# A one-layer decoder: batch 0's residual, norm and queries moved up; the experts' down projections in three passes; rows of the experts' blocks loaded by two engines

## The chip, the cores and the metric

The kernel runs on one core of one Trainium2 chip. The metric is the device time of one execution in microseconds; lower is better. The time before is the median of three runs.

## The reference

The layer has a width D of 256, 16 heads of 16, 32 sequences of 112 tokens, and a context of 375 positions for each sequence. All is float32:

```python
x = x + self_attention(layernorm(x))        # causal, window of 64
x = x + cross_attention(layernorm(x), ctx)  # bias by relative position, 375 keys
x = x + experts(layernorm(x))

# experts: 8 of them, each token goes to its best two
probs = softmax(xf @ router_w.T); keep the top 2, normalise them
g = xf @ gate_w[e] + gate_b[e]; u = xf @ up_w[e] + up_b[e]
h = silu(g) * u                              # 512 wide
y = sum over the two experts of prob * (h @ down_w[e] + down_b[e])
```

## The kernel before

Each engine runs its own instruction stream, and all streams are made from one list of steps. A step is a name and a batch number (`("x1", 0)`), and it stands for one piece of work on one engine; semaphores tie the streams together. `order(B)` builds the list: a periodic order for the 32 batches (`PERIOD`), then an order written out by hand for the end of the attention part and the first part of the experts (`TAIL_ORDER`).

**Attention, about the first 865 us.** Per batch: norm, queries and keys, masked scores in four groups (`sm0` to `sm3` on VectorE, 16 small reductions with the mask, and `su` on GpSimd behind them), values, output projection (`wo`), residual (`x1`), norm (`ln2`, `rs2` on GpSimd, `xn2` on ScalarE), its transpose (`x2T`, copied by `x2Tc`) and the cross queries (`q2`, split into a rounded high part by `q2m` on ScalarE and a low part by `q2l` on VectorE). The two halves of the queries are then paired by a DMA (`qx`), without which the first cross scores (`S0`) can't start. The cross keys (`k0`, `k1`) are split in the same way by `k0c` and `k1c` (ScalarE) and `k0l` and `k1l` (VectorE). The steps of these small products take the two PSUM banks A and B in turn, in the order of the list; a step waits until the one that had the bank before it is drained. For `k0` and `k1` that is when `k0l` and `k1l` are done. `split_weights` splits the context's weights, once, at step `cl` of batch 0.

**Experts.** Token rows are scattered to DRAM by expert (`sc`), and read back in blocks of 128 rows that all belong to one expert. The first 42 blocks (`NFULL`) are worked on in 21 pairs (`NP`), the last 21 one by one. `blocks:n` are small VectorE steps that compute the table of blocks. `get` and `add_and_load` on GpSimd load the rows of a block into one of `XB` = 12 buffers; `add` adds a block's result to the output in DRAM by an indirect DMA, which waits until the results before it have landed. Per pair k, TensorE transposes the rows of pair k+1, does the gate product (step `bg`), the up product (`bu`) and then the down product of pair k-1 (`down_pair`, L916). Gate and up products of a pair run in the format fp32r: weights and rows are each split into a high part (ScalarE copies it) and a low part (VectorE subtracts), and three products (`PASSES`: high x high, low x high, high x low) make up one float32 product (L901). The down product is a plain float32 product, which the trace shows as two instructions each. In the last 21 blocks all three products are plain float32 (L866, L876). VectorE weighs the result (`weigh_rows`, L1420) into one of two buffers `y2`. TensorE's down product waits in the next round until VectorE has read the last one (`s_yw`).

The order of VectorE in a pair is: `weigh_pair`, the up weights' low part, the low part of the next rows, and in step `bu` the next gate weights' low part and four multiplications into `hidden_rows`. ScalarE: the up weights' high part, the copy of the next rows, the activation of the gate, the next gate weights' high part, the weighted bias.

## Time and profile before

| what | us |
|---|---|
| median of 3 runs | 1214.28 (1214.12 to 1214.49) |
| the profiled execution, its own time | 1211.85 |
| its span | 1210.2 |
| TensorE busy (matmul) in the span | 1168.2 (97%) |
| VectorE, ScalarE, GpSimd busy | 868.3, 753.8, 821.0 |

The profile is of one execution. Its table in 40 slices has TensorE at nine tenths or more from the third slice on but for one; the stages before and after differ in what the other engines do beside it.

### The profile page before, as it was taken

The page shows a single profiled execution, that of the slowest core. Times are in us where ns is not written, and L with a number is a line of the kernel's source. Part 1 is how long each engine was busy: PE and PEld are TensorE (multiplying, and loading weights), DVE is VectorE, ACT ScalarE, POOL GpSimd, SP SyncE. Part 2 cuts the span into 40 slices and gives each one's busy share as a digit, 9 for nine tenths or more (in the row PEclk, how much of TensorE's full clock was granted, in tenths as well). Part 3 has the DMA queues.
Part 4 walks back from the last instruction along what each step waited for, and adds up shares of the span by engine and source line. Part 5 has one row for each costly group of instructions (what it writes and reads, how often), then busy time and mean ns, then how long its engine had stood idle before and what let it go on. Part 6 is the DMA issues. An engine that isn't in the chain of part 4 may idle for free.

```text
span 1210.2 us, 36900 instructions
## 1 busy us (share of the span) xinstructions
PE 1168.2 (97%) x12874; PEld 1023.7 (85%) x12874; DVE 868.3 (72%) x3851; ACT 753.8 (62%) x1845; POOL 821.0 (68%) x1593
## 2 busy tenths in 40 slices
PE   6899999999999999999999999999899999999996
PEld 4688888888888888888888888887689999998995
DVE  3567888888888888888888888888777655544442
ACT  2567766767766767766766766766564555555552
POOL 4677788778788778788778788876636644444432
PEclk8999999999999999999999999999899999999998
DMA  8411122121122121112112112122765433333221
GB/s 191 93 43 47 50 59 75 50 58 58 51 58 75 50 58 58 51 59 75 52 58 59 51 58 71 48 65 87 230 212 140 76 57 54 53 58 56 46 32 23
DMA packets 70936, 86.11 MB, mean 71 GB/s; under 512 B 25600, under 2 KB 57728, under 8 KB 70752
## 3 DMA queue, kind: packets, MB, share of 16 engines
q1 hardware_dynamic: 54768, 58.60, 16.7%
q0 software_dynamic: 15552, 25.05, 10.7%
q8 instruction: 105, 1.72, 0.6%
q14 instruction: 79, 0.65, 0.2%
q10 hardware_dynamic: 432, 0.10, 0.0%
HBM read 43.10 MB, written 20.95 MB: 53 GB/s over the span
## 4 chain that ended last, share of the span: by engine, by line
PE 90%; DVE 4%; issue 2%; POOL 2%; DMA 1%; ACT 0%; POOLq 0%; DVEq 0%
PE bank_S L901 10%; PE bank_Q L824 7%; PE bank_P L824 6%; PE bank_Q L916 5%; PE bank_S L815 5%; PE bank_S L866 5%; PE bank_B L737 4%; PE bank_A L737 4%; PE bank_B L837 4%; PE bank_A L837 3%; PE bank_A L804 3%; PE bank_P L763 3%; PE bank_B L804 3%; PE bank_Q L876 3%; PE bank_B L796 3%; PE bank_S L754 3%
## 5 line engine op out<-in xcount | busy, mean ns | idle before, releaser
L628 POOL TENSOR_SCALAR arena<-arena,mC 112x375 f32<-112x375 f32 x512 | 297.6, 594 | 26.4 <-DVE mC L1282 24.3
L1282 DVE CUSTOM_DVE_ANT_0 arena<-bank_S,arena 112x375 f32<-112x375 f32 x512 | 260.4, 543 | 56.9 <-PE bank_P L824 30.4
L634 POOL TENSOR_SCALAR arena<-arena 112x112 f32<-112x112 f32 x512 | 175.0, 356 | 85.3 <-DVE arena L1270 85.3
L654 POOL DMA_INDIRECT out<-y,xb x63 | 106.6, 1692 | 83.8 <-DVE y L1420 48.6
L824 PE MATMUL bank_Q<-ident,arena 112*126 112x112 f32 x858 | 131.9, 262 | 2.1 <-POOL arena L628 1.5
L1071 ACT ACTIVATE pTC<-bank_P 126x336 f32<-126x336 f32 x226 | 102.6, 454 | 40.6 <-PE bank_P L824 16.9
L1270 DVE CUSTOM_DVE_ANT_0 arena<-bank_S,arena 112x112 f32<-112x112 f32 x512 | 102.1, 270 | 14.6 <-PE bank_S L754 14.6
L1071 ACT ACTIVATE pTC<-bank_Q 126x336 f32<-126x336 f32 x222 | 101.3, 456 | 18.1 <-PE bank_Q L824 14.6
L824 PEld LDWEIGHTS bank_Q<-ident,arena 112*126 112x126 f32 x858 | 96.2, 141 | 15.4 <-issue 9.7
L824 PE MATMUL bank_P<-ident,arena 112*126 112x112 f32 x678 | 107.9, 268 | 1.3 <-ACT pTC L1071 0.8
L647 POOL DMA_DIRECT2D xb<-xs x63 | 44.1, 700 | 80.1 <-issue 76.6
L824 PEld LDWEIGHTS bank_P<-ident,arena 112*126 112x126 f32 x678 | 74.7, 140 | 26.1 <-issue 16.1
L641 POOL DMA_INDIRECT xs<-x,pos x64 | 65.6, 1025 | 26.1 <-issue 22.3
L815 PE MATMUL bank_S<-k,q 32*112 32x376 f32 x1024 | 77.1, 374 | 3.7 <-issue 2.7
L916 PE MATMUL bank_Q<-arena,hidden_rows 128*128 x336 | 76.0, 379 | 0.0
L916 PEld LDWEIGHTS bank_Q<-arena,hidden_rows 128*128 128x128 f32 x336 | 62.4, 190 | 7.6
L1431 DVE TENSOR_TENSOR gwR_low<-arena,gwR_high 128x1024 fp32r<-128x1024 f32 x21 | 26.1, 1243 | 48.4 <-ACT gwR_high L1120 45.0
L614 POOL TENSOR_TENSOR rstd<-rstd,power 112x1 f32<-112x1 f32 x96 | 54.6, 568 | 8.0
L613 POOL TENSOR_SCALAR rstd<-mv 112x1 f32<-112x1 f32 x96 | 22.3, 233 | 55.5 <-DVE mv L1250 50.4
L1410 DVE SCALAR_TENSOR_TENSOR hidden_rows<-bank_S,gub,gates 128x128 f32<-128x128 f32 x84 | 23.7, 345 | 48.7 <-PE bank_S L866 42.4
L815 PEld LDWEIGHTS bank_S<-k,q 32*112 32x112 f32 x1024 | 35.4, 170 | 27.2 <-issue 21.0
L1035 ACT ACTIVATE arena<-bank_A 128x224 f32<-128x224 f32 (+2 forms) x102 | 43.6, 428 | 19.8 <-PE bank_A L745 7.7
(263 smaller groups left out, 3566.9 us busy)
## 6 DMA issues: line engine op xcount, KB each, us to landing
arena<-in_l_ctxT SPq DMA_DIRECT2D x32, 378.0 KB, 3.5
k<-k_low SPq DMA_DIRECT2D x64, 188.0 KB, 2.3
xb<-xs POOLq DMA_DIRECT2D x63, 129.0 KB
q<-q SPq DMA_DIRECT2D x64, 112.0 KB
arena<-in_L_ffn_gate_w SPq DMA_DIRECT2D x8, 512.0 KB
arena<-in_L_ffn_up_w SPq DMA_DIRECT2D x8, 512.0 KB
arena<-in_L_ffn_down_w SPq DMA_DIRECT2D x8, 512.0 KB
arena<-in_x SPq DMA_DIRECT2D x32, 112.0 KB, 2.0
```

Of the source, the lines that this page charges most:

```text
L628: pool.tensor_scalar(z[n % NZ][:, 0:T], z[n % NZ][:, 0:T], -1.0, mC[:, n:n + 1], ALU.mult, ALU.add).then_inc(s_u, 1)
L634: m = pool.tensor_scalar(sF[r][:, j, :], sF[r][:, j, :], -1.0, mF[:, r, j:j + 1], ALU.mult, ALU.add)
L654: pool.indirect_dma_start(out=out[:, :], out_offset=bass.IndirectOffsetOnAxis(ap=xb[x][:, D + 1:D + 2].bitcast(I32), axis=0), in_=y2[x % 2 ...
L737: m = pe.matmul(dst, xt[:, c, :], w[:, c, 0:n], start=(c == 0), stop=(c == DC - 1))
L815: m = pe.matmul(bank[f"S{r}"][0:S, 0:T + 1], q2[b % 2][32 * r:32 * r + 32, u, c, p, :], k2[b % 2][32 * r:32 * r + 32, c, p, :], start=u == ...
L824: m = pe.transpose(B_[0:TP, t * S:(t + 1) * S], z[n % NZ][:, t * TP:(t + 1) * TP], ident[0:S, 0:S])
L837: m = pe.matmul(B_[32 * r:32 * r + HP, 0:S], v2[b % 2][:, t, n, :], pTC[n % NZ][:, t, :], start=(t == 0), stop=(t == TC - 1))
L901: m = pe.matmul(bk[f // 2][:, f % 2 * 2 * P:(f % 2 + 1) * 2 * P], wR[part][w][:, c, f * P:(f + 1) * P], xbR[k % 2][u][:, c, :], start=(c = ...
L916: m = pe.matmul(bankY[:, h * D:(h + 1) * D], hidden_rows[k % 2][:, c, h * P:(h + 1) * P], w[:, c, :], start=(c == 0), stop=(c == FC - 1))
L1071: act.activation(pTC[n % NZ][:, :, :], v3(B_, TC, S, TP), ACT.Exp).then_inc(drain_sem(f"p{n}", b), 1)
L1270: m = dve.tensor_tensor_reduce(out=sF[r][:, j, :], in0=t[:, j, :], in1=window[:, :], scale=1.0, scalar=3.0e38, op0=ALU.add, op1=ALU.min, a ...
L1282: dve.tensor_tensor_reduce(out=z[n % NZ][:, 0:T], in0=bank[f"S{r}"][0:S, 0:T], in1=nbias[:, n, :], scale=1.0, scalar=3.0e38, op0=ALU.add, ...
```

## The change

1. **Beginning.** A table `BEGINNING` moves nine steps of batch 0 in the list: `rs2`, `x1`, `ln2`, `xn2`, `x2Tc`, `q2m`, `q2l`, `q2` and `x2T`. `split_weights` moves from `cl` to `nrm` of batch 0, and the copy of a constant from batch 0's `x1` to batch 1's.
2. **Down products in three passes.** The down weights and the hidden values are split into high and low parts as the others are. One buffer of each (`wR["dw"]`, `hR`), and one `hidden_rows` where there were two. Blocks 42 and 62 keep the plain product.
3. **Loads.** 10 row buffers where there were 12. GpSimd loads the rows for the first four pairs' adds (`SEAM` = 8), then SyncE does it. Odd pairs up to 17 write their results to `xbT`, so that there are four result buffers.
4. **Order of the end.** `warm` (the first gate weights' split) and the transpose `x3T` of batch 30 go behind the last softmax steps and `pv3`; the block table's parts are spread over more pairs, one in each.

Cut to its core:

```diff
-XB = 12
+XB = 10
+SEAM = 8
+BEGINNING = (("rs2", 0, ("su3", 1)), ("x1", 0, ("sm3", 1)), ("ln2", 0, ("sm3", 1)), ("xn2", 0, ("k1c", 0)),
+             ("x2Tc", 0, ("k1c", 0)), ("q2m", 1, ("k1c", 0)), ("q2l", 1, ("k1l", 0)), ("q2", 1, ("k1", 0)), ("x2T", 1, ("k1", 0)))
 def order(B):
+    for word, behind, anchor in BEGINNING:
+        steps.remove((word, 0))
+        steps.insert(steps.index(anchor) + behind, (word, 0))
...
-p15 e14 warm pv2 oc1 e15 p13 oc2 p12 e13 pf:-2 e12 pkg:10 ... pfD:-2 rcB:-2
-x3T:-1 x3Tc:-1 pv3 oc3 bt otc ...
+p15 e14 pv2 oc1 e15 p13 oc2 p12 e13 pf:-2 e12 warm pkg:10 ... pfD:-2 rcB:-2 pv3 oc3 x3T:-1
+x3Tc:-1 bt otc ...
...
+            hR = [sb(f"hR_{part}", [P, FC, 2 * P], F32R, st) for part in ("high", "low")]
+            rows_out = [[y2[h] if k % 2 == 0 or k > NP - 4 else xbT[h] for h in range(2)] for k in range(NP)]
@@ SyncE
+                    def load_behind(j):
+                        sp.wait_ge(s_add, 16 * (j - (j > NFULL)))
+                        for n in (j + XB - 2, j + XB - 1) if j < NFULL else (j + XB - 2,):
...
+                                load_rows(n)
...
@@ TensorE
                     def down_pair(k):
-                        pe.wait_ge(s_hh, 2 * k + 2)
+                        pe.wait_ge(s_dw, k + 1)
+                        pe.wait_ge(s_hl, k + 1)
...
-                                m = pe.matmul(bankY[:, h * D:(h + 1) * D], hidden_rows[k % 2][:, c, h * P:(h + 1) * P], w[:, c, :],
+                                for u, w in PASSES:
+                                    m = pe.matmul(bankY[:, h * D:(h + 1) * D], hR[u][:, c, h * P:(h + 1) * P],
...
@@ ScalarE, step bg
+                    def hidden_high(k):
+                        act.wait_ge(s_hh, 2 * k + 2)
+                        if k:
+                            act.wait_ge(s_y, 2 * k)
+                        act.activation(hR[0][:, :, :], hidden_rows[:, :, :], ACT.Copy).then_inc(s_hi, 1)
...
+                            if b:
+                                hidden_high(b - 1)
+                                weights_high(b - 1, "dw", s_y)
                             for half in range(2):
                                 silu_pair(b, half)
@@ VectorE, step bg
                                 copy_low(b + 1)
+                            if b:
+                                hidden_low(b - 1)
+                                weights_low(b - 1, "dw", s_dw, 1)
...
@@ VectorE, single blocks
                     for j in range(NFULL, NBLK):
                         if j == NFULL:
                             weigh_pair(NP - 2)
+                            hidden_low(NP - 1)
+                            weights_low(NP - 1, "dw", s_dw, 1)
+                        elif j > NFULL + 1:
+                            down_low(j - 1)
                         if j + 1 < NBLK:
                             weights(j + 1)
                         hidden(j)
...
@@ VectorE, weigh_rows
-                        if j >= 2:
-                            dve.wait_ge(s_add, 16 * (j - j % 2 if j < NFULL else max(j - 1, NFULL)))
+                        if j >= NFULL:
+                            dve.wait_ge(s_add, 16 * max(j - 1, NFULL))
+                        elif j // 2 > NP - 3:
+                            dve.wait_ge(s_add, 16 * (j - j % 2))
+                        elif j >= 4:
+                            dve.wait_ge(s_add, 16 * (j - j % 2 - 2))
```

## Rows read from the trace of the kernel before

**Rows 1.** The page's first part: busy us, share of the span, instructions.
```profile
PE 1168.2 (97%) x12874; PEld 1023.7 (85%) x12874; DVE 868.3 (72%) x3851; ACT 753.8 (62%) x1845; POOL 821.0 (68%) x1593
```
**Rows 2.** Windows: length, busy PE, PEld, DVE, ACT, POOL, PEclk, DMA share, GB/s.
```profile
929.31:1064.37 135.06, 135.06 (x954) 128.56 (x953) 80.04 (x147) 73.04 (x127) 72.54 (x63) 1.00 0.37 63
```
**Rows 3.** The chain that ended last, one pair: start us, us, what.
```profile
987.19 3.46 PE bank_Q L916 x16
991.09 5.75 PE bank_S L901 x48
996.84 3.46 PE bank_Q L916 x16
```
**Rows 4.** The same chain, one single block.
```profile
1103.31 3.57 PE bank_S L866 x32
1106.88 1.73 PE bank_Q L876 x8
```
**Rows 5.** Timeline of DVE over one pair; in brackets the idle time before.
```profile
986.62 1.23 DVE L1431 TENSOR_TENSOR gwR_low<-arena,gwR_high 128x1024 fp32r<-128x1024 f32 x1 [2.97 <-ACT gwR_high L1120]
987.76 1.65 DVE L1442 SCALAR_TENSOR_TENSOR hidden_rows<-bank_S,gub,gates 128x256 f32<-128x256 f32 x4
990.69 0.88 DVE L1420 SCALAR_TENSOR_TENSOR y<-bank_Q,xb,dbw 128x256 f32<-128x256 f32 x2 [1.27 <-PE bank_Q L916]
991.48 1.22 DVE L1431 TENSOR_TENSOR uwR_low<-arena,uwR_high 128x1024 fp32r<-128x1024 f32 x1
992.61 0.68 DVE L1425 TENSOR_TENSOR xbR_low<-bank_P,xbR_high 128x512 fp32r<-128x512 f32 x1
```
**Rows 6.** Timeline of ACT in the same stage.
```profile
994.99 1.06 ACT L1120 ACTIVATE gwR_high<-arena 128x1024 fp32r x1
...
1000.77 0.60 ACT L1114 ACTIVATE xbR_high<-bank_P 128x512 fp32r<-128x512 f32 x1 [2.74 <-PE bank_P L888]
```
**Rows 7.** Timeline of DVE: first and last of five steps of one table part.
```profile
935.39 0.20 DVE L1370 TENSOR_TENSOR ge<-lower,nf 1x64 f32<-1x64 f32 x1
...
936.26 0.23 DVE L1375 TENSOR_TENSOR diff<-offs 1x8 f32<-1x8 f32 x1
```
**Rows 8.** Timeline of DVE in the first pairs.
```profile
923.93 0.88 DVE L1420 SCALAR_TENSOR_TENSOR y<-bank_Q,xb,dbw 128x256 f32<-128x256 f32 x2 [2.13 <-DMA out<-y,xb]
```
**Rows 9.** Timeline of POOL: adds (L654) and a load (L647).
```profile
1001.70 2.17 POOL L654 DMA_INDIRECT out<-y,xb  x1 [0.42 <-DVE y L1420]
...
1060.51 1.66 POOL L654 DMA_INDIRECT out<-y,xb  x1 [0.30 <-issue]
...
1067.55 0.60 POOL L647 DMA_DIRECT2D xb<-xs  x1 [3.49 <-issue]
```
**Rows 10.** Timeline of PE: the down product of block 43.
```profile
1095.58 1.99 PE L876 MATMUL bank_Q<-arena,hidden_rows 128*128 x8 [1.77 <-DVE y L1420]
```
**Rows 11.** Timeline of DVE at the beginning.
```profile
30.35 0.27 DVE L1270 CUSTOM_DVE_ANT_0 arena<-bank_S,arena 112x112 f32<-112x112 f32 x1
...
33.47 0.33 DVE L1470 CAST before<-x 112x112 fp32r<-112x112 f32 x1
33.83 0.42 DVE L1471 TENSOR_TENSOR x<-bank_A,arena 112x256 f32<-112x256 f32 x1
...
41.10 0.69 DVE L1487 SCALAR_TENSOR_TENSOR q<-bank_A,q 128x224 fp32r<-128x224 f32 x2 [3.39 <-ACT q L1053]
```
**Rows 12.** Timeline of PE at the beginning.
```profile
31.39 1.09 PE L737 MATMUL bank_A<-arena 128*112 128x256 f32 x4 [0.30 <-ACT arena L1035]
...
34.40 0.41 PE L796 MATMUL bank_A<-cT_high,wkv_high 128*128 128x376 f32 x1 [0.89 <-DVE x L1471]
...
45.85 0.61 PE L815 MATMUL bank_S<-k,q 32*112 32x376 f32 x8 [2.71 <-issue]
```
**Rows 13.** Windows of 1 us, PE alone: length, busy us, PEclk, DMA share, GB/s.
```profile
23.00:24.00 1.00, 0.40 (x16) 1.00 0.97 126
24.00:25.00 1.00, 0.99 (x24) 0.50 1.01 146
```

More of the change, by code:

```diff
@@ L397, in decoder_layer @@
             s_xb = [sem(f"block_loaded{i}") for i in range(XB)]
+            s_xs = [sem(f"block_loaded_by_sp{i}") for i in range(XB)]
             s_bX = sem("block_transposed")
@@ L407, in decoder_layer @@
             s_xh = sem("block_high_ready")
-            s_wh = {w: sem(f"{w}_high_ready") for w in ("gw", "uw")}
+            s_wh = {w: sem(f"{w}_high_ready") for w in ("gw", "uw", "dw")}
+            s_dw = sem("down_weights_split")
+            s_hi = sem("hidden_high_ready")
+            s_hl = sem("hidden_low_ready")
             s_db = sem("down_bias_weighted")
@@ L469, in decoder_layer, with rows_loaded @@
             filled_last = {n: max(k for m, k in place.values() if m == n) + 1 for n in "ABPQS"}
+            def rows_loaded(j):
+                first = SEAM + XB - 2
+                return (s_xb[j % XB], 16 * (j // XB + 1)) if j < first else (s_xs[j % XB], 16 * ((j - first) // XB + 1))
             held = {}
@@ L583, in _ @@
                             load_package(sp, e, half)
+                        elif step == "add" and b >= SEAM and b % 2 == 0:
+                            load_behind(b)
+                    for j in range(1 + max(b for step, b in steps if step == "add"), NBLK):
+                        if j >= NFULL or j % 2 == 0:
+                            load_behind(j)
                     sp.wait_ge(s_add, 16 * NBLK)
@@ L1119, in weights_high @@
                             act.wait_ge(used, 2 * k)
-                        act.activation(wR[part][0][:, :, :], package(e, part).rearrange("p (c f) -> p c f", c=DC), ACT.Copy).then_inc(s_wh[part], 1)
+                        act.activation(wR[part][0][:, :, :], package(e, part).rearrange("p (c f) -> p c f", f=parts[part][1] // (
+                            FC if part == "dw" else DC)), ACT.Copy).then_inc(s_wh[part], 1)
                     def silu_pair(k, half):
@@ L1232, in _ @@
                     for j in range(NFULL, NBLK):
+                        if j == NFULL:
+                            hidden_high(NP - 1)
+                            weights_high(NP - 1, "dw", s_y)
                         if j == NFULL:
@@ L1430, in weights_low @@
                         dve.wait_ge(s_wh[part], k + 1)
-                        dve.tensor_tensor(wR[part][1][:, :, :], package(e, part).rearrange("p (c f) -> p c f", c=DC), wR[part][0][:, :, :].bitcast(F32), ALU.subtract).then_inc(then, n)
+                        dve.tensor_tensor(wR[part][1][:, :, :], package(e, part).rearrange("p (c f) -> p c f", f=parts[part][1] // (
+                            FC if part == "dw" else DC)), wR[part][0][:, :, :].bitcast(F32), ALU.subtract).then_inc(then, n)
                     def hidden_pair(k, half):
@@ L1462, in _ @@
                         elif step == "nrm":
+                            if b == 0:
+                                split_weights()
                             if b:
@@ L1478, in _ @@
                         elif step == "cl":
-                            if b == 0:
-                                split_weights()
                             need(dve, s_ch, b + 1)
```

128 lines of the change are left out of this document (81 added, 47 removed).

## The prediction

> **What bounds the kernel now.** I read the page first: TensorE is busy for 97% of the span [rows 1], so the time is TensorE's work plus a few holes. Then the windows by stage. In the pair stage TensorE is busy all of 135.06 us, VectorE 80.04 of them (59%), ScalarE 73.04 [rows 2]. Then the chain of waits, which in that stage is TensorE alone: per pair 3.46 us of down product in 16 instructions, 5.75 us of gate and up products in 48, and 9.65 us from one down product to the next [rows 3]. A single block has 3.57 us of gate and up and 1.73 us of down [rows 4]. The two rows of a pair are a price list: the float32 down product has 8 products of 256 columns in 3.46 us, 0.43 us each; an fp32r product of the same 256 columns takes 5.75 / 48 = 0.12 us. Last I read VectorE's, ScalarE's and GpSimd's timelines over a pair for what stands in between [rows 5, 6, 9], and all engines' at the holes: 2.71 us before the first cross scores of batch 0 [rows 12], 1.77 us at block 43 [rows 10].
>
> **Down products in three passes.** A pair's down product becomes 24 fp32r products, 24 x 0.12 = 2.88 us for 3.46: 0.58 us less. The stationary side changes with each one, as in the rows the price is from. A single block's becomes 12 x 0.12 = 1.44 for 1.73: 0.29 us less, in 19 blocks (43 to 61), 5.5 us. The new period of a pair is 9.65 - 0.58 = 9.07 us, if TensorE stays the bound.
>
> Does it? VectorE's starts in a pair are 1.14 us apart for a low part of 128x1024, 1.57 for the four multiplications, 0.79 for weighing, 0.60 for the next rows [rows 5]; with two low parts more it has 4 x 1.14 + 1.57 + 0.79 + 0.60 = 7.5 us of 9.07. A table part adds up to 1.1 us [rows 7], in pairs 3 to 12, one each: 8.6 us. ScalarE's two more copies at 1.06 [rows 6] bring it from 5.2 (73.04 x 9.65 / 135.06) to 7.3 us. So neither is the bound by load, but the order must hold too. I set time 0 at the end of `bu`. The down product of pair k-1 ends at 2.9. VectorE weighs at 3.1 to 3.9, up weights to 5.0, rows to 5.7, and then comes `hidden_low(k)`, which needs `hidden_high(k)`: that waits for the down product (one buffer), sits behind the copy of the next rows (transposes at 3.3, copy to 4.1) and ends at 5.1; the weights' high part ends at 6.1. The low parts end at 6.9 and 8.0. TensorE comes to the down product at 9.07. The slack is 1.0 us. Behind it ScalarE has the activations and the gate weights' high part, which it ends at 8.8, so VectorE's gate weights go from 8.9 to 10.0, the multiplications to 11.6, and it can weigh at 12.2 (9.07 + 3.1): 0.5 us of slack. The 2.97 us in which VectorE waits for ScalarE now [rows 5] are the cover that the new work uses up. With a table part it is 0.5 us late, which the slack of 1.0 holds. Where that cover is gone each pair costs what it lacks. From the down product of pair 4 to that of pair 19 are 15 periods: 15 x 0.58 = 8.7 us less, and 0.6 for pair 20.
>
> **The first pairs.** There VectorE also has batch 31's routing. Beside its own order the new 2.3 us (two low parts) stand ahead of work that TensorE waits for: the up weights of pair 3 come about 1.3 us later, of pair 4 about 1.8. Against it go five cheaper down products (2.9 us), and waits of VectorE for a landed add, of which 2.13 us is the longest [rows 8]: with four result buffers they go. The swap of `x3T` and `pv3` lets `pv3` go ahead of the wait for the routing's bank, but `x3T` and behind it the first transposes of rows now wait for VectorE's first gate weights and the slot counts: the first gate product about 1 to 2 us later, half of it absorbed by VectorE's later waits. I follow the streams step by step with the durations above and get the down product of pair 4 ending 0.5 us later than before. Bounds: 3 us earlier (all down savings kept) and 4 us later (all of 2.3 us in two pairs lost).
>
> **Loads and adds.** GpSimd's cycle in a pair was two loads and two adds: from the first add to the first load behind it, which waits for both to land, 1067.55 - 1060.51 = 7.04 us [rows 9]; with the two loads behind it (0.60 each and their gaps) that is near 9, and would have been the next bound at 9.07. Without the loads it is 7.0 and 0.9 for weighing. SyncE has nothing else to do there and loads four pairs ahead, after the adds that free the buffers: nothing on the path. 10 buffers for 12 cost nothing while a load has two periods of lead.
>
> At the seam to the single blocks the result buffers are two again. From the end of pair 19's down product TensorE gets to that of block 43 in 3 x (3.57 + 0.2) + 2.88 + 1.73 = 15.9 us. The adds' chain needs 0.2 + 0.9 + 7.04 (pair 19), 0.1 + 0.9 + 7.04 (pair 20), 0.1 + 0.5 for weighing block 42, which is 16.8; and `down_low(43)` is queued on VectorE behind that weighing, 0.6 + 1.14 us more. So block 43 stalls some 2.7 us where it stalled 1.77 [rows 10]: 0.9 us lost. Bounds: 0 and 2.5.
>
> The Trainium skill ("SBUF — State Buffer", section "SBUF: two separate sides") has VectorE with two SBUF inputs and GpSimd share one port, which one of them holds for a whole instruction. The trace has a sign of it: an add issued while the up weights' low part ran took 2.17 us, others 1.66 [rows 9]. By that rule both adds of a pair can be 0.5 us longer, since VectorE now has four such instructions; 8.9 of 9.07 us, still hidden, and 1 us more at the seam, which is within its bounds.
>
> **The beginning.** The residual needs `wo`, which ends at 31.39 + 1.09 = 32.5 [rows 12]; now it starts at 33.83, after 16 masked reductions from 30.35 to 33.47 [rows 11]. Moved ahead of them it starts at 32.5: 1.3 us earlier, and VectorE stands idle before it. The norm ends at 33.6. The reductions (3.1 us) then end at 36.7, and `k0l` is queued behind them: 37.2, for about 35.4 now. But `x2T` takes bank B, which `k0` holds until `k0l`; so it runs at 37.2, its copy ends at 38.1. `k1c` is queued on ScalarE behind that copy (39.0), `k1l` follows (39.5), and `q2` takes bank A, which waits for `k1l`. `q2` and its high part take 1.8 us: `q2l` at 41.3, against 41.10 now [rows 11]. The queries come no sooner. TensorE meanwhile is idle from 34.5 to 37.2 and from 37.6 to 39.5, 4.6 us, with `qk` of batch 2 and the rest queued behind; it loses the holes of 0.89 (before `k1`) and 2.71 us [rows 12]. Net 1.0 us later at the first scores: 46.9 for 45.85. `split_weights` runs in VectorE's idle time before `nrm` and moves nothing, since `k0` comes at 32.1 for other reasons.
>
> Then the clock. After some us in which it was busy half of the time (0.40 us of the last one) the granted clock went from 1.00 to 0.50, 2.4 to 1.2 GHz [rows 13]. The new hole is emptier than that: 0.4 us of work in 5. If it falls, the 5 us of work behind it run at half speed and 2.4 us more are lost. I take 2.5 us for the whole of the beginning, bounds -1.5 (the queries 1.3 us earlier and no new hole) and 3.5.
>
> The Trainium skill ("TensorE: Matmul & The Clock Gate", section "HAM oscillation — how this bites in real kernels") says that a wait that is long enough makes the next stretch start at the low clock. By that rule the beginning costs the 3.5 us and not 1.0, and the sum would be 1204.4; it speaks against this part of the change, and the row of the fall agrees.
>
> **The sum.** First pairs 0.5, pairs -8.7 - 0.6, seam 0.9, single blocks -5.5, beginning 2.5: -10.9 us. The end is unchanged (two adds in a row behind block 62). From the profiled execution's 1211.85 that is 1201.0; the median of the runs is 2.4 above it, so 1203.4. I say 1203.
>
> **Rivals.**
> - *The beginning does what it is arranged for.* For it: VectorE reaches the residual 1.3 us earlier. Against: the banks of `k0` and `k1`. It gives 1203.4 - 4.0 = 1199.
> - *VectorE bounds the pairs.* For: 8.6 of 9.07 us in ten pairs, and waits for ScalarE between. Against: 1.0 us of slack. If each of the 15 periods is 0.3 us short: 1208.
> - *The single buffers of the split down operands, slower than before.* `hidden_high` can't start until the down product before has been read, and the low parts must end before the next: 5.1 us of chain in a window of 6.2. The price is whatever the chain has beyond 6.2, in 20 pairs. It decides against the kernel when the chain is over 6.2 + 10.9 / 20 = 6.7 us. If VectorE's wait of 2.97 us for ScalarE comes to lie ahead of the low parts and half of it is not hidden, the chain is 7.2 and the time 1203.4 + 20 x 1.0 = 1223. Against: those parts are queued ahead of that wait.
> - *The passes do not issue at 0.12 us.* If the down product saves nothing (passes at 0.144), 1203.4 + 14.8 = 1218. Against: the 48 products of a pair in the same form at 0.12 [rows 3].
>
> **The numbers.** Forecast (within 1200.5 to 1206.5) 0.6; the beginning pays 0.16; VectorE bounds 0.15; single buffers 0.05; passes 0.04. 0.2% is 2.4 us, about what a measurement here can tell from no change. Faster takes the first three, 0.91; slower 0.06 and the same 0.03, from the last two. The range is 1197 to 1209.
>
> **What would show it.** Right: down products of 256 columns at 0.12 us, down products 9.07 us apart from pair 5 on, 5.2 us per single block, a stall of 2 to 3 us at block 43, the first scores of batch 0 at 46 us or later with TensorE idle before `x2T` and `q2`. Wrong: `down_pair` waiting for a low part in each pair (then VectorE or the buffers bound), no hole before 40 us, or the period still near 9.65.

## The result, and the profile after

The changed kernel takes 1209.16 us (1207.66 to 1209.87, 7 runs), the kernel before on the same chip 1214.28 (1212.47 to 1215.72): ratio 0.9957, 95% interval 0.9945 to 0.9968. It is faster, by 5.1 us and not by 11, and the time lies outside the range. The profiled execution has a span of 1206.4 us, 3.8 less than before.

Cuts through both traces say where the 3.8 us come from. A mark that both traces have is the last norm of heads, which ends the attention stage but for one batch (timeline of VectorE, before, then after):

```profile
852.88 0.25 DVE L1256 RECIPROCAL rt<-bank_A 112x16 f32<-112x16 f32 x1
```
```profile
858.95 0.25 DVE L1321 RECIPROCAL rt<-bank_A 112x16 f32<-112x16 f32 x1
```

It is 6.1 us late. From it to the start of pair 4's down product are 80.2 us for 76.3 (939.20 and 929.15): 4.0 us late, and 3.4 by the end of that product (942.08 and 932.61), which is what the forecast was for. From its end to the kernel's are 264.3 us for 277.6: 13.3 us gained, against 13.9 forecast (-8.7 - 0.6 + 0.9 - 5.5). So 6.1 + 3.4 - 13.3 = -3.8. The sum was nearly right in these four terms and wrong at the beginning and in the first pairs.

The 13.3 us are 8.7 in 15 pairs, 0.2 from there to block 43 (0.3 lost was forecast) and 5.4 in the single blocks, less 1.0 behind the last down product, where the forecast had the end unchanged. A second profile of the same kernel (the unfilled one of the filled stretches, below) has 6.2 us, then 5.3 at the start of pair 4's down product, and 13.2 gained behind it. So the parts are told to 1 or 2 us.

**The part that was nearly right.** The page's first part (as [rows 1]), then the window over 14 pairs (as [rows 2]), then the chain over one pair (start us, us, what; as [rows 3]):

```profile
PE 1153.2 (96%) x13118; PEld 1022.5 (85%) x13118; DVE 951.2 (79%) x3931; ACT 811.3 (67%) x1925; POOL 823.2 (68%) x1546
```
```profile
939.36:1066.33 126.97, 126.97 (x1066) 126.97 (x1066) 112.86 (x185) 95.03 (x155) 73.01 (x37) 1.00 0.41 69
```
```profile
997.08 5.76 PE bank_S L939 x48
1002.84 2.88 PE bank_Q L954 x24
```

14 pairs take 126.97 us, 9.07 each, and TensorE is busy in all of them. The 24 passes take 2.88 us, 0.12 each. VectorE rose from 59% to 89% of the stage (112.86 of 126.97), ScalarE to 75%: the cover is nearly used up, but it holds. VectorE over one pair (as [rows 5]):

```profile
997.54 1.22 DVE L1502 TENSOR_TENSOR uwR_low<-arena,uwR_high 128x1024 fp32r<-128x1024 f32 x1
998.68 0.68 DVE L1496 TENSOR_TENSOR xbR_low<-bank_P,xbR_high 128x512 fp32r<-128x512 f32 x1
999.28 1.22 DVE L1521 TENSOR_TENSOR hR_low<-hidden_rows,hR_high 128x1024 fp32r<-128x1024 f32 x1
1000.41 1.22 DVE L1502 TENSOR_TENSOR dwR_low<-arena,dwR_high 128x1024 fp32r<-128x1024 f32 x1
1002.26 1.22 DVE L1502 TENSOR_TENSOR gwR_low<-arena,gwR_high 128x1024 fp32r<-128x1024 f32 x1 [0.63 <-ACT gwR_high L1172]
```

The 2.97 us wait for ScalarE of [rows 5] is down to 0.63, and the two new low parts stand where it was. GpSimd's two adds of that pair (as [rows 9]):

```profile
998.06 2.13 POOL L700 DMA_INDIRECT out<-y,xb  x1 [2.55 <-DVE y L1491]
1000.49 2.55 POOL L700 DMA_INDIRECT out<-y,xb  x1 [0.30 <-issue]
```

An add takes 2.13 and 2.55 us where a free one took 1.66, hidden as forecast. At the seam VectorE and TensorE at block 43 (as [rows 10]):

```profile
1093.88 0.48 DVE L1491 SCALAR_TENSOR_TENSOR y<-bank_Q,xb,dbw 128x256 f32<-128x256 f32 x1 [2.46 <-DMA out<-y,xb]
1094.29 0.68 DVE L1527 TENSOR_TENSOR hR_low<-hidden_rows,hR_high 128x512 fp32r<-128x512 f32 x1
1094.88 1.22 DVE L1530 TENSOR_TENSOR dwR_low<-arena,dwR_high 128x1024 fp32r<-128x1024 f32 x1
1096.16 0.39 PE L913 MATMUL bank_Q<-dwR_high,hR_high 128*128 128x256 f32 x1 [2.05 <-DVE dwR_low L1530]
```

The weighing waits for a landed add, the low parts are queued behind it, and TensorE waits 2.05 us (forecast 2.7, before 1.77). Behind it a block takes 5.22 us for 5.52.

One thing changed at the end that the forecast did not have. GpSimd's adds in the single blocks, in this trace and in the second profile of the same kernel:

```profile
1162.85 1.97 POOL L700 DMA_INDIRECT out<-y,xb  x1 [3.26 <-DMA out<-y,xb]
```
```profile
1159.67 1.54 POOL L700 DMA_INDIRECT out<-y,xb  x1 [3.82 <-DVE y L1491]
```

In this trace the adds of the single blocks take 1.5 to 2.3 us, and from block 43's on nearly every one waits for the one before it to land: the chain that ended last runs over them from the seam to the end (8% of the span). TensorE waits for nothing in these blocks, since adds and products both take 5.2 us each, but the kernel ends 16.4 us after the start of the last down product, for 15.4 before. In the second profile TensorE is 1.6 us later, behind a fall of the clock at block 43; there nearly all adds take 1.54 us and wait for VectorE, and the end is 15.6 us behind. The add at 1162.85 starts while VectorE's low part of the down weights runs (1162.18 to 1163.41), the one at 1159.67 just ahead of it (1159.79). So the single blocks have two chains of the same length.

**The beginning.** TensorE and the windows of 1 us (as [rows 12, 13]):

```profile
39.16 0.41 PE L760 MATMUL bank_B<-ident,arena 112*128 112x112 f32 x2 [2.72 <-DVE k_low L1581]
41.36 2.05 PE L818 MATMUL bank_A<-arena 128*128 128x112 f32 x8 [1.78 <-DVE k_low L1581]
43.20 3.62 PE L774 MATMUL bank_B<-arena 128*128 128x112 f32 x16
51.39 0.60 PE L844 MATMUL bank_S<-k,q 32*112 32x376 f32 x8
```
```profile
39.00:40.00 1.00, 0.41 (x2) 0.98 0.00 0
40.00:41.00 1.00, 0.00 (x0) 0.50 0.00 0
43.00:44.00 1.00, 1.00 (x6) 0.50 0.85 299
```

The two idle stretches are as the prediction had them, 1.9 us later, each behind a low part of the keys (VectorE, as [rows 11]), and the clock fell to 1.2 GHz behind them: the 16 products at 43.20 take 3.62 us, 1.95 at 2.4 GHz. The first scores start at 51.39 for 45.85; the forecast was 46.9, and 2.4 more if the clock fell.

```profile
19.87 1.26 DVE L1412 TENSOR_TENSOR wkv_low<-arena,wkv_high 128x1024 fp32r<-128x1024 f32 x1
28.73 0.26 DVE L1321 RECIPROCAL arena<-bank_A 112x16 f32<-112x16 f32 x1 [7.60 <-PE bank_A L810]
...
34.41 0.42 DVE L1559 TENSOR_TENSOR x<-bank_A,arena 112x256 f32<-112x256 f32 x1 [4.11 <-PE bank_A L766]
38.57 0.54 DVE L1581 TENSOR_TENSOR k_low<-bank_B,k 128x376 fp32r<-128x376 f32 x1
```

The residual, meant to come 1.3 us earlier, starts at 34.41 for 33.83: the norm of heads ahead of it is at 28.73 (26.84 before). The split of the weights now runs at 19.2 to 21.1, beside GpSimd's masked shifts, which take 6.92 us here:

```profile
16.48 6.92 POOL L680 TENSOR_SCALAR arena<-arena 112x112 f32<-112x112 f32 x16 [0.79 <-DVE arena L1335]
```

and 5.44 before. They take 6.9 us in all five profiles that have the split at its new place, and 5.4 to 5.5 in all others. The Trainium skill ("SBUF — State Buffer", section "SBUF: two separate sides") has a port that both engines share; by that rule a VectorE instruction with two SBUF inputs beside a GpSimd one makes one wait for the other, and the rows agree.

**The first pairs.** ScalarE, VectorE and TensorE at the end of the attention stage:

```profile
871.47 1.06 ACT L1172 ACTIVATE gwR_high<-arena 128x1024 fp32r x1 [0.50 <-DMA arena<-in_L_ffn_down_b]
...
872.75 1.23 DVE L1502 TENSOR_TENSOR gwR_low<-arena,gwR_high 128x1024 fp32r<-128x1024 f32 x1 [3.22 <-ACT gwR_high L1172]
...
875.19 0.41 PE L760 MATMUL bank_B<-ident,x 112*128 112x112 f32 x2 [3.35 <-DVE run L1386]
877.52 0.58 PE L939 MATMUL bank_S<-xbR_high,gwR_high 128*128 128x256 f32 x1 [0.36 <-DVE xbR_low L1496]
...
915.08 0.36 PE L939 MATMUL bank_S<-xbR_high,uwR_high 128*128 128x256 f32 x1 [1.99 <-issue]
```

The gate weights' high part is now behind the last exponentials, the low part waits 3.22 us for it, the slot counts (`run`) stand behind the low part, and TensorE waits 3.35 us for them. The first gate product (877.52; 869.77 before) comes 18.6 us behind the mark for 16.9: 1.7 us. From it to pair 4's down product are 61.7 us for 59.4: 2.3 us, though four down products in it are 0.58 us cheaper each. TensorE stands idle for 6.5 us of it, for 3.4 before: it waits for late up and gate weights, 1.99 us in the row at 915.08 (VectorE's up weights end at 914.99).

### The profile page after: what moved, and what is told of

Its sections match the earlier page's. It is cut to its first block, busy times and chain, and to the rows that moved or that the text cites. A ratio compares the mean times of both kernels' runs of the same rounds, so it can differ in the third digit from the quotient of the medians.

```text
span 1206.4 us, 37394 instructions
## 1 busy us (share of the span) xinstructions
PE 1153.2 (96%) x13118; PEld 1022.5 (85%) x13118; DVE 951.2 (79%) x3931; ACT 811.3 (67%) x1925; POOL 823.2 (68%) x1546
## 4 chain that ended last, share of the span: by engine, by line
PE 82%; DMA 10%; issue 3%; DVE 2%; POOL 1%; ACT 1%; SPq 0%; POOLq 0%; DVEq 0%; ACTq 0%
PE bank_S L939 10%; DMA out<-y,xb 8%; PE bank_Q L853 7%; PE bank_P L853 6%; PE bank_S L844 5%; PE bank_Q L954 5%; PE bank_A L766 4%; PE bank_B L766 4%; PE bank_B L866 4%; PE bank_A L866 3%; PE bank_A L833 3%; PE bank_P L792 3%; PE bank_B L833 3%; PE bank_B L825 3%; PE bank_S L783 3%
## 5 line engine op out<-in xcount | busy, mean ns | idle before, releaser
L680 POOL TENSOR_SCALAR arena<-arena 112x112 f32<-112x112 f32 x512 | 177.6, 367 | 78.4 <-DVE arena L1335 78.4
L700 POOL DMA_INDIRECT out<-y,xb x45 | 94.7, 2105 | 105.8 <-DMA out<-y,xb 58.8
L700 POOL DMA_INDIRECT out<-xbT,xb x18 | 40.1, 2227 | 27.7 <-DVE xbT L1491 20.8
L792 PE MATMUL bank_P<-ident,arena 112*112 112x112 f32 x376 | 52.8, 263 | 2.5 <-POOL arena L680 2.0
L1211 ACT ACTIVATE arena<-bank_P 112x448 f32<-112x448 f32 x94 | 51.7, 550 | 2.7 <-PE bank_P L792 1.9
L939 PE MATMUL bank_S<-xbR_high,gwR_high 128*128 128x256 f32 x168 | 50.3, 299 | 3.0 <-issue 2.7
L1074 ACT ACTIVATE arena<-bank_B 128x448 f32<-128x448 f32 (+2 forms) x91 | 38.7, 425 | 20.7 <-PE bank_B L774 11.1
```

Source lines behind the costliest of these rows:

```text
L680: m = pool.tensor_scalar(sF[r][:, j, :], sF[r][:, j, :], -1.0, mF[:, r, j:j + 1], ALU.mult, ALU.add)
L700: pool.indirect_dma_start(out=out[:, :], out_offset=bass.IndirectOffsetOnAxis(ap=xb[x][:, D + 1:D + 2].bitcast(I32), axis=0), in_=rows_out ...
L792: m = pe.transpose(d[:, j, :], sF[r][:, j, :], ident[0:S, 0:S])
L939: m = pe.matmul(bk[f // 2][:, f % 2 * 2 * P:(f % 2 + 1) * 2 * P], wR[part][w][:, c, f * P:(f + 1) * P], xbR[k % 2][u][:, c, :], start=(c = ...
```

## The experiments

All times are medians; a ratio is to the kernel before on the same chip, with its 95% interval. "The mark" is the norm of heads above.

**Nothing moved at the beginning.**

```diff
-BEGINNING = (("rs2", 0, ("su3", 1)), ("x1", 0, ("sm3", 1)), ...
+BEGINNING = ()
```

> The changed kernel with batch 0's residual, norm, transposes and queries back in their old places (nothing moved at the beginning; the weights are still split ahead of batch 0's norm of heads). In the changed kernel the first cross scores come at 51.39 us instead of 45.85, and the whole attention stage behind them is 6.08 us late. My theory: of these, about 1.9 us arise before the norm of heads (VectorE splits the weights beside GpSimd's masked shift, which took 6.92 us for 5.44) and stay here; the other 4 us are the idle stretches that the move makes (before the second transposes and before the queries, some 2 us net) and the low clock behind them (2 us), and go. So the attention stage is 1.9 us late against the kernel before instead of 6.08, and the time is 1205.2 (1209.2 - 4). Rival A, the move only shifts holes and the price is all the weights' split: the time stays within 1 us of 1209. Rival B, both are one late chain that ends at GpSimd: all 6 us go, 1203.

Measured: 1204.26 us, 0.9904 (0.9884 to 0.9924). All but 0.5 us of what undoing both parts gives (below). The mark is at 855.20, 3.8 us earlier than in the changed kernel, and as early as with both parts undone (855.27): the 1.9 us that should have stayed are not seen there.

**The weights' split at its old place**, `split_weights()` back in the step `cl`.

> The changed kernel with the splitting of the weights back at its old place behind batch 0's context rows; the moved steps stay moved. My theory: GpSimd's masked shift, which holds VectorE's and its own shared way into SBUF, is back at 5.4 us from 6.9, the norm of heads starts at 26.8 us instead of 28.7, and the kernel gains 1.9 us: 1207.3. But the split (1.9 us of VectorE) then stands behind the residual and in the way of the moved chain, so up to 1 us of it can be lost again. Rival A, the fall of the clock is what costs and it does not depend on the split: no change, 1209. Rival B, the split at its new place is what makes all 6 us: 1203.

Measured: 1207.72 us, 0.9936 (0.9919 to 0.9954); the mark is at 856.67, 2.3 us earlier. The medians say 1.4 us and the ratios 2.5 (1.9 expected); the intervals overlap.

**Both undone** (the base of what follows).

> The changed kernel with both parts of the beginning undone: the order of batch 0's steps and the place of the split as in the kernel before. My theory: the first 260 us are those of the kernel before (first cross scores at 45.85 us within 0.3), the whole 6.08 us go, and the rest of the change keeps its -9.9 us against the kernel before: 1203.1, about what the prediction said for the whole change. Rival, the later start of the attention stage is partly absorbed further on (a stage bound by transfers takes it up): then less comes back than 6.08 us, 1205 to 1207.

Measured: 1203.71 us, 0.9901 (0.9881 to 0.9921), 1203.1 expected. In this profile the first scores are at 46.70 and not within 0.3 of 45.85, and the mark is at 855.27 for 852.88 in the kernel before, whose order it has (last section). The rest of the change is worth 1%, 12 us, and the beginning gives 6 or 7 of them away (0.9957 and, measured again, 0.9948, less 0.9901).

**The beginning alone**, put into the kernel before.

> The kernel before with the beginning of the changed kernel alone (steps moved, weights split ahead of batch 0's norm of heads), the down products and everything behind as before. My theory: it is slower than the kernel before by the 6.1 us that the attention stage of the changed kernel is late: 1220.4. Rival, the fill of SBUF or the queues of the changed kernel have a part in the delay, and without them the beginning costs what the prediction gave it, 2.5 us or less: 1216.8.

Measured: 1218.45 us, 1.0034 (1.0016 to 1.0051): slower, by 4.1 us (3.2 by the medians). The mark is at 857.38, 4.5 us late, not 6.1. So the beginning is slower than before with nothing else changed. Its size is not settled: the interval is 1.9 to 6.2 us, and holds the theory's 6.1 and the rival's 2.5.

**The changed kernel again, and the same with TensorE kept busy in the two idle stretches.**

```diff
+for i in range({("x2T", 0): 10, ("q2", 0): 7}.get((step, b), 0)):
+    pe.matmul(bank["P"][:, 0:P], ident[:, :], ident[:, :], start=True, stop=True)
 B_, F_ = fill_wait(pe, step, b), fill_sem(step, b)
```

> The changed kernel again, as the base of the two runs beside it: 1209 us, ratio 0.9957 within 0.002.

> The changed kernel with 10 and 7 extra products (128 columns, float32, results never read) ahead of batch 0's second transposes and of its queries, where TensorE is idle for 2.72 and 1.78 us: they fill most of the idle time (2.1 and 1.5 us) and lie on nobody's path. My theory: the granted clock then stays at 1.00 from 37 to 47 us, the queries and the queries and keys of batch 2 take 1.06 and 1.8 us for 2.05 and 3.62, and the kernel gains 2.5 us: 1206.7. Rival A: the clock falls all the same, since the stretch ahead of the queries comes behind one that fell at 22.9 us: no gain, 1209. Rival B: behind it other waits (the scores of batch 0 wait for the self-attention of batch 1) take the gain up: clock up, but less than 1 us gained.

Measured: 1208.81 us, 0.9948 (0.9935 to 0.9962), and 1206.05 us, 0.9931 (0.9916 to 0.9946). Windows of TensorE (length, busy us, PEclk, DMA share, GB/s), unfilled, then filled:

```profile
38.00:40.00 2.00, 0.39 (x2) 0.87 0.00 0
40.00:42.00 2.00, 0.24 (x2) 0.50 0.00 0
42.00:44.00 2.00, 1.97 (x9) 0.50 0.27 95
```
```profile
38.00:40.00 2.00, 1.79 (x16) 1.00 0.14 44
40.00:42.00 2.00, 2.00 (x21) 1.00 0.44 148
42.00:44.00 2.00, 2.00 (x20) 1.00 0.63 156
```

The clock stays at 2.4 GHz and the median is 2.8 us lower, 2.5 expected; the intervals overlap, so the size is not closely known. The traces have the first scores at 45.85 for 51.50. Of these 5.6 us 3.4 are there before the first filled product (the residual is at 31.44 for 34.85, behind other falls of the clock), and only 2.2 arise behind the residual, where the filling is. That the clock does not fall there is the filling's doing. (The Trainium skill, "TensorE: Matmul & The Clock Gate", section "HAM oscillation — how this bites in real kernels", has a long wait make the next stretch start at the low clock; the two traces agree.)

**Residual and norm alone moved**, weights split in the old place.

```diff
+BEGINNING = (("rs2", 0, ("su3", 1)), ("x1", 0, ("sm3", 1)), ("ln2", 0, ("sm3", 1)))
```

> The changed kernel with the weights split in the old place and only batch 0's residual and norm moved ahead of batch 1's masked reductions; the transposes, queries and their copies stay where they were. With all of the steps moved this beginning cost 4.2 us over none. My theory: TensorE's idle stretches come from the moved transposes and queries, whose banks wait for the low parts of the keys; without them nearly all of the 4.2 us go: 1204 to 1204.5. Rival: the masked reductions, 1.1 us later behind the residual, and GpSimd's part of the norm behind them are what costs: 1206 or more.

Measured: 1207.02 us, 0.9934 (0.9914 to 0.9953); 1204 to 1204.5 expected. By the ratios nearly the whole cost of the moved steps (0.9936) is there without the moved queries, and my theory fell; the six executions lie 6 us apart, so this is not sharp. TensorE's queries and keys of batch 2:

```profile
36.85 3.75 PE L773 MATMUL bank_B<-arena 128*128 128x112 f32 x16 [2.72 <-DVE k_low L1580]
```

They wait 2.72 us for the low part of batch 0's keys, and behind the wait they run at the low clock (3.75 us). On VectorE that low part is behind the 16 reductions, which the residual has pushed back.

**That low part ahead of the reductions too.**

```diff
+BEGINNING = (("rs2", 0, ("su3", 1)), ("x1", 0, ("sm3", 1)), ("ln2", 0, ("sm3", 1)), ("k0l", 0, ("sm3", 1)))
```

> The run with residual and norm alone moved (1207.0 us), with the low part of batch 0's first half of keys moved ahead of the masked reductions as well, so that on VectorE it does not wait for them (3.1 us). My theory: this low part is what TensorE waits 2.72 us for; it then comes at about 34 us for 36.25, the wait goes or falls below 0.5 us, the clock stays up (the products of queries and keys of batch 2 take 1.95 us, not 3.75), and the kernel is back at that of the undone beginning: ratio 0.990 to 0.991, 1203.5. Rival: the reductions, 1.5 us later still, hold GpSimd's shifts and batch 1's scores: the wait moves to these, ratio 0.993 as before.

Measured: 1204.88 us, 0.9909 (0.9892 to 0.9926); 0.990 to 0.991 expected. The low part, then the product:

```profile
32.32 0.55 DVE L1580 TENSOR_TENSOR k_low<-bank_B,k 128x376 fp32r<-128x376 f32 x1 [0.90 <-ACT k L1099]
...
32.93 2.04 PE L773 MATMUL bank_B<-arena 128*128 128x112 f32 x16 [0.50 <-DVE k_low L1580]
```

The wait is 0.50 us for 2.72, and the product runs at the high clock, 2.04 us for 3.75. So one instruction's place in VectorE's queue makes this wait. That it also makes the difference between 0.9934 and 0.9909 is likely and not shown: the intervals overlap, and of the 5.5 us by which the first scores are earlier (44.62 for 50.12) 1.8 are there at the residual already. The moved residual still gains nothing over 0.9901.

**The first gate weights split earlier**, on the base (`warm` back ahead of `pv2`).

> From here on the base is the changed kernel with its beginning undone (1203.71 us); this one also has the splitting of the first expert's gate weights back ahead of the exponentials, where the kernel before has it. In the base TensorE is idle for 3.33 us before the routing's transposes at 871.71, which wait for VectorE's slot counts, and these stand behind the low part of the gate weights (869.27, itself 3.21 us late behind ScalarE's high part). My theory: with the high part some 8 us earlier the slot counts run as soon as their product is there, the idle time is 1 us or less, the first gate product comes 2 us earlier, and the time is 1201.7. Rival A: ScalarE's high part (1.9 us) then delays the exponentials and so the values of the last group by as much: no gain, 1203.7. Rival B: the first pairs are bound by VectorE, and it absorbs the earlier start: 1203.7 with the first gate product 2 us earlier all the same.

Measured: 1201.39 us, 0.9899 (0.9878 to 0.9921): by the ratio not told apart from the base. The trace tells: VectorE's low part and TensorE's transposes are

```profile
864.68 1.23 DVE L1501 TENSOR_TENSOR gwR_low<-arena,gwR_high 128x1024 fp32r<-128x1024 f32 x1 [0.68 <-issue]
...
867.19 0.41 PE L759 MATMUL bank_B<-ident,x 112*128 112x112 f32 x2 [0.86 <-DVE run L1385]
```

and the first gate product comes 17.2 us behind the mark (19.4 in the base), pair 4's down product 78.5 (80.6). The 2.1 us arrive whole in this profile; rivals A and B fall by it. The first gate product is at 17.2 to 17.5 us in all four profiles with the early split and at 18.6 to 20.4 in the others of the changed kernel; pair 4's down product varies more (80.0 in the run of the better parts, whose order up to there differs from this one only in the transposes). Some 0.8 us are lost again in this profile by the kernel's end, behind block 43, where the clock fell (last section).

**The whole end of the attention stage in the old order** (`x3T x3Tc` ahead of `pv3` too).

> As the run before, and the routing's transposes and their copy back ahead of the last values too, so the whole end of the attention stage has the order of the kernel before. My theory: the first gate product stands to the start of the stage as in the kernel before; against the run with the weights alone it gains 0.5 us or nothing: 1201.2 to 1201.7. Rival: the swap of transposes and values was itself the loss (the transposes take a bank that waits for the slot counts), so that only this run gains and the one with the weights alone does not.

Measured: 1200.33 us, 0.9889 (0.9870 to 0.9909). From the mark the first gate product is at 17.2 us again, pair 4's down product at 79.0: no gain of the swap by itself is seen, and the place of the gate weights has one. With the old order TensorE waits 2.1 us for the rows of batch 31 ahead of their transposes (0.5 in the run before); ScalarE is late with them behind GpSimd's part of the norm. No run here says what delays that.

**Narrow low parts in pairs 0 to 3**: 2 columns wide, the down products of the high parts only (24 as before). It leaves out the correction in these pairs, and since all three passes then take high x high, it adds that product three times: their results are not usable, their times are.

```diff
+n = 2 if k < 4 else 2 * P        # hidden_low; weights_low of "dw" alike
+hR[u * (k > 3)], wR["dw"][w * (k > 3)]   # down_pair
```

> The base with the two new low parts on VectorE 2 columns wide in pairs 0 to 3, and these pairs' down products all of the high parts (24 as before): it leaves out the correction of the first four pairs and takes some 2 us of VectorE's work out of each. My theory for the first pairs: the down product of pair 4 comes 2 to 2.5 us late because each pair's low parts stand ahead of batch 31's routing and of the next up weights; without them the down product of pair 4 comes at least 2 us earlier, and the time is 1201.5. Rival A, ScalarE's high parts (1.1 us each, kept here) or the order of the tables is what delays: no gain, 1203.7. Rival B, all of the loss is before the first gate product: no gain either.

Measured: 1198.94 us, 0.9871 (0.9854 to 0.9887). From the first gate product to pair 4's down product are 56.9 us for 61.2 (61.6 in another profile of the same code): 4.3 to 4.7 us, twice what I expected. Without the low parts the stretch is 2.5 us shorter than before (59.4), about the 2.3 us of the four cheaper down products in it. So the low parts in VectorE's queue take all of that and some 2 us more. TensorE's idle time in the stretch is 4.0 us, for 5.9 and 6.6 in the two others.

**Block 43's low parts ahead of the weighing of block 42.**

```diff
-elif j > NFULL + 1:
+elif j > NFULL + 2:
     down_low(j - 1)
...
+if j == NFULL + 1:
+    down_low(j)
```

> The base with one block's low parts moved: those of block 43 ahead of the weighing of block 42's rows, which waits 2.46 us for a landed add. My theory: TensorE's wait of 2.05 us at the down product of block 43 shrinks to 0.4 us and the time to 1202.1. Rival: behind the seam the adds into the output, one every 5.2 us beside TensorE's 5.2 us per block, are the chain that ends last; then the wait at block 43 goes but comes back in later blocks, and the time stays at 1203.7.

Measured: 1200.96 us, 0.9891 (0.9874 to 0.9909). TensorE waits 0.85 us instead of 2.06, and from block 42's down product to the last one are 100.4 us for 101.6: 1.2 us, with nothing given back, since the kernel ends 16.4 us behind the last one's start for 16.3. By the ratio it is not told apart from the base. The rival fell in that the wait does not come back; but in this trace too nearly every add waits for the one before it to land. The adds are level with TensorE; whether they would hold up a block shorter than 5.2 us, no run tried.

**One pass in the pairs' down products** (`for u, w in PASSES[:1]`).

> The base (changed kernel, beginning undone) with one pass (high part with high part) for three in the down products of the pairs; it leaves out 16 of 24 products of each, and all operands are still split. TensorE then has 9.07 - 16 x 0.12 = 7.15 us of work in a pair, and the period shows the next bound, that is how much of the 9.07 us VectorE, ScalarE and GpSimd really leave. My theory (the prediction's loads): VectorE with 7.5 us, 8.6 with a table part, is next: periods of 7.6 to 8.6 us, some 1.0 us less per pair on the mean, 1188. Rival A, GpSimd's two adds with the weighing between them (7.0 + 0.9): 7.9 us in every pair. Rival B, the chain over the single buffers of the down operands leaves nothing: the period stays above 8.9.

Measured: 1189.56 us, 0.9794 (0.9773 to 0.9815). 14 periods from pair 4 on take 114.5 us, 8.18 each; the fifteenth takes 10.45, with a wait of 2.80 us for the down weights' low part. They are 8.3 to 8.6 us in the pairs with a table part and 7.49 in the three behind these, where VectorE's queue has no gap (in the last ones it waits for ScalarE's gate weights, 0.63 and 1.35 us, and they take 7.6 to 8.7). From one gate low part to the next:

```profile
1009.53 1.21 DVE L1500 TENSOR_TENSOR gwR_low<-arena,gwR_high 128x1024 fp32r<-128x1024 f32 x1
...
1017.02 1.21 DVE L1500 TENSOR_TENSOR gwR_low<-arena,gwR_high 128x1024 fp32r<-128x1024 f32 x1
```

7.49 us, and the prediction's sum of VectorE's starts was 7.5. VectorE is the next bound, at 7.5 to 8.6 of 9.07. The chain over single buffers does not hold a pair at 8.9 us or more, and GpSimd's adds do not hold it at 7.9: three periods are shorter.

**GpSimd loads the rows of the pairs** (SEAM = 34).

> The base with GpSimd loading the pairs' rows up to row block 41, as in the kernel before, instead of SyncE from block 16 on; all else as in the base. My theory (the prediction's): GpSimd's cycle in a pair is then two adds (7.04 us to the next load), two loads and the weighing, 8.9 to 9.1 us, beside a period of 9.07: up to 0.1 us per pair is lost, 1203.7 to 1205.5. Rival A: with four result buffers the adds have a pair of slack and nothing is lost. Rival B: the loads block GpSimd for longer than 0.6 us each (they wait for both adds to land), the cycle is 9.65 or more, and the whole gain of the pairs goes: 1212.

Measured: 1206.76 us, 0.9943 (0.9921 to 0.9966), 0.004 over the base with intervals that touch. Three of the 15 periods from pair 4 on are 9.4 to 9.7 us; in sum the trace has 137.2 us for 135.8. It is the fastest of the four executions (1203.55), and shows 1.4 us of the 5 that the ratios give; where the rest is, it doesn't say. GpSimd over one pair:

```profile
998.18 1.65 POOL L699 DMA_INDIRECT out<-y,xb  x1 [0.30 <-issue]
1000.14 1.59 POOL L699 DMA_INDIRECT out<-y,xb  x1 [0.30 <-issue]
...
1005.22 0.59 POOL L692 DMA_DIRECT2D xb<-xs  x1 [2.20 <-issue]
...
1007.25 1.66 POOL L699 DMA_INDIRECT out<-xbT,xb  x1 [0.30 <-issue]
```

From add to add are 9.07 us with no slack but the wait for landing. GpSimd's cycle is as long as the period, as forecast, and the loads on SyncE are worth 1.4 us in this trace.

**The better parts together**: base, old order at the end of the attention stage, block 43's low parts early.

> What the runs so far point to, together: the down products in three passes and the loads as in the changed kernel, the beginning and the end of the attention stage in the order of the kernel before, and block 43's low parts ahead of the weighing of block 42. If the parts add (1200.3 with the old order at the end of the attention stage, 1.2 us from the low parts of block 43): 1199.1. Rival: at the seam the wait of 2.0 us sometimes lowers TensorE's clock and costs 1.6 us more (it did in two profiles of four); without the wait that goes too: 1198.3.

Measured: 1199.65 us, 0.9876 (0.9855 to 0.9896), near what the parts add up to (1199.1). In its trace TensorE waits 1.43 us at block 43, not 0.85, and the clock doesn't fall there.

**The same with the down products of pairs 0 to 3 in float32.**

```diff
+if k < FIRST:        # FIRST = 4: rows and weights as they are, no hidden_low, no low part of "dw";
                     # the hidden values of odd pairs go to a second buffer, as in the kernel before
+    m = pe.matmul(bankY[:, h * D:(h + 1) * D], rows[:, c, h * P:(h + 1) * P], w[:, c, :], ...)
```

> The same with the down products of pairs 0 to 3 in float32 as in the kernel before (no splitting in them), in three passes from pair 4 on. If VectorE's low parts are what makes the first pairs late (with tiny ones the down product of pair 4 came 3.6 us earlier from the stage's end), then this gains 3.6 less 4 x 0.58 of longer down products, 1.3 us: 1197.8 to 1198. Rival: ScalarE's high parts count too, and it gains 2 us or more: 1197 or less. Rival: the float32 down products need their weights for longer, and the next package or the next rows wait for them: no gain.

Measured: 1197.92 us, 0.9859 (0.9835 to 0.9882). It beats both kernels, by 17 us and by 11; that it beats the run before it is not shown (the intervals overlap). The traces don't settle it. From the first gate product to pair 4's down product are 61.7 us for 62.8, but the run with the old order at the end of the attention stage, whose code is that of the run before there, has 61.8. TensorE's idle time in the stretch is 4.1 us for 9.4; against it stand four down products that are 0.58 us longer, and the clock, which is low at its start here and not there (windows of this run, then of the run before it):

```profile
868.00:872.00 4.00, 3.95 (x20) 0.50 0.92 328
```
```profile
868.00:872.00 4.00, 3.33 (x30) 1.00 0.85 257
```

## Why the prediction was wrong

- *Pairs, seam, single blocks* (-8.7, -0.6, +0.9, -5.5): right in mechanism and near in size, 13.9 us forecast and 13.3 measured. The load of VectorE (7.5 and up to 8.6 us) was measured with one pass, GpSimd's cycle of 9 with its loads put back: both as forecast. "The end is unchanged" was put at nothing, with a look at the last two adds alone: it is 1.0 us longer in this trace, where the adds go one behind the other through all single blocks. That the seam came out 0.5 us better than forecast hides half of it, by luck.
- *"I take 2.5 us for the whole of the beginning"*: the term was mis-sized, and it is the larger part of the miss; it is 6.1 us in the trace and 0.5 to 0.6% of the time by the ratios. The mechanism was the forecast's, low parts behind the reductions and then the low clock. Two steps failed. The clock was taken at 1.5 us of its price of 2.4; the two groups of products behind the stretch take 2.7 us more, (3.62 - 1.95) + (2.05 - 1.06), and filling it gave 2.8 by the medians. And "`split_weights` ... moves nothing": by itself it moves nothing that the ratios tell (0.9904 against 0.9901), but GpSimd's shifts are 1.5 us longer beside it, the norm of heads is 1.9 us later and the residual with it (34.41 for the forecast 32.5), and with the moved steps in place it costs 1.4 to 2.5 us more by two runs whose intervals overlap. At the first scores 1.0 (forecast) + 1.9 + 2.7 are 5.6 us, and 5.5 were measured.
- *"The down product of pair 4 ending 0.5 us later"*: mis-sized, 3.4 us. The first gate product is 1.7 us late, as forecast (1 to 2), and this is the place of the first gate weights; but of "half of it absorbed" nothing is seen in the run that put them back (2.1 us at both ends). And the low parts' delays were counted as 1.3 and 1.8 us; they cost 4.3 to 4.7 us in all, against 2.9 us of cheaper products. 1.7 + 4.3 to 4.7 - 2.9 is 3.1 to 3.5. Why they cost that much is read from the traces: in these pairs VectorE has routing of batch 31 in the same queue, and TensorE then waits for gate and up weights.
- *Rivals*: "the beginning does what it is arranged for" fell (slower alone, 1.0034). "VectorE bounds the pairs" fell where the forecast had it, in pairs 4 to 19; something like it holds in pairs 0 to 3, where TensorE waits for VectorE's low parts. Single buffers and passes over 0.12 us fell.
- The chances: 0.91 for faster was borne out. The range of 1197 to 1209 holds both upper bounds at once (beginning 3.5, first pairs 4: 1203.4 + 1.0 + 3.5 = 1207.9). The first pairs stayed within theirs, 3.4 of 4; the beginning did not, 6.1 of 3.5.

## What to carry to other kernels

An engine's queue is in order: a small instruction that frees a bank (0.55 us here), left behind a block of work that was pushed back, can cost more than the move gains. Look for it before moving the block, and move it too. Where a change opens idle stretches in TensorE, count the low clock behind them in full. Where work is moved to an idle time of its engine, look at what GpSimd does beside it. Count the load of an engine stage by stage: a split that is free in the steady stage can bound the few iterations in which older work is still in the queue.

## What the runs showed of the hardware

The wait of about 2 us at block 43 lowered the clock in some profiles and not in others of nearly the same code. In the run with the gate weights split earlier, then in the one with block 43's low parts early (wait 0.85 us):

```profile
1088.00:1090.00 2.00, 1.02 (x6) 0.87 0.49 126
1090.00:1092.00 2.00, 2.00 (x12) 0.50 0.58 74
1092.00:1094.00 2.00, 2.00 (x16) 0.78 0.01 2
```
```profile
1088.00:1090.00 2.00, 1.15 (x10) 1.00 0.13 35
1090.00:1092.00 2.00, 2.00 (x20) 1.00 0.48 109
```

In nine profiles a wait there (1.94 to 2.31 us, and 2.87 with one pass) was followed by 1.2 GHz, with a next block of 6.6 to 6.9 us for 5.2; in four others it was not, with waits of 1.98, 2.05, 2.06 and 2.20 us. In the three with block 43's low parts early (0.85, 0.85 and 1.43 us) the clock stayed up. The same code is on both sides: 2.05 us without a fall in one profile of the changed kernel, 1.94 with one in the other. A fall there costs 1.6 us in the next block and some 0.7 us by the kernel's end: from block 42's down product to the end are 117.9 to 118.4 us in the four profiles without one, and 118.6 to 119.0 in eight with one (all but the one with one pass).

The beginning varies as well. Nine profiles whose kernels have the same beginning (the base and those built on it) have the mark between 851.91 and 855.27 us; in the latest the clock was low for some 5 us from 49 us on, and the first scores come 2.2 us later than in the earliest. So what the clock does behind such a wait is a chance rather than a price, and a difference of 2 or 3 us between single profiles says nothing on an edit.
